# Dummy products on TensorE behind the key transposes, behind the counts of expert 0's search and ahead of the first list

## The reference

```
x = x + attention(layernorm(x), ctx, ctx)           # one head, D = 256, softmax over 256 keys
t = layernorm(x).reshape(4096, 256)
S = sigmoid(t @ Wg).T                               # 8 experts x 4096 rows
G, I = top_k(S, 1024)                               # each expert takes its 1024 best rows
hid = gelu(t[I] @ W1[e] + b1[e])                    # 256 -> 1024
out = (hid @ W2[e] + b2[e]) * G                     # 1024 -> 256
x = x + zeros.at[I].add(out)
```

## Time and profile before

| what | us |
|---|---|
| median of 3 runs (lowest, highest) | 510.77 (509.81, 510.78) |
| the profiled execution, its own time | 514.28 |
| its span in the trace | 512.5 |
| key transposes on TensorE start | 126.62 |
| first list written (`ids`) | 149.25 |
| first product of expert 0 on TensorE | 159.87 |
| first Gelu of expert 0 on ScalarE | 168.14 |

### The profile page before, as it was taken

The page is one execution under the profiler, slowest core; times in us unless marked ns, Lnnn a source line. Parts: engine busy times, 40 slices in busy tenths (PEclk is TensorE's granted clock), DMA queues, the critical chain, the costliest instruction groups (busy, mean ns, idle before and its releaser), DMA issues.

```text
span 512.5 us, 10717 instructions
## 1 busy us (share of the span) xinstructions
PE 481.5 (94%) x3806; PEld 347.7 (68%) x3807; DVE 334.1 (65%) x765; ACT 317.2 (62%) x607; POOL 287.0 (56%) x392
## 2 busy tenths in 40 slices
PE   7899999998357999999999999999999999999995
PEld 6688888877235558648747845864874784685484
DVE  6788999978874888675385465547538546535721
ACT  3777777866781782594387188259439618836920
POOL 1758999996324067546625726745662572773044
PEclk9999999999556999999999999999999999999998
DMA  7730766566803556547717916834761781683024
GB/s 223 234 114 2 232 179 165 142 187 182 241 16 100 178 126 104 103 130 136 139 35 202 163 22 194 171 48 135 137 132 52 188 160 22 187 105 41 2 33 50
DMA packets 91946, 64.21 MB, mean 125 GB/s; under 512 B 53060, under 2 KB 87816, under 8 KB 91912
## 3 DMA queue, kind: packets, MB, share of 16 engines
q1 hardware_dynamic: 78992, 46.41, 33.0%
q0 software_dynamic: 12288, 17.05, 20.9%
q10 hardware_dynamic: 632, 0.31, 0.2%
HBM read 35.83 MB, written 16.91 MB: 103 GB/s over the span
## 4 chain that ended last, share of the span: by engine, by line
PE 86%; DVE 5%; ACT 4%; issue 2%; DMA 1%; POOL 1%; POOLq 0%; SPq 0%; DVEq 0%; ACTq 0%
PE bank L1247 78%; PE bank L1254 2%; PE bank L1267 1%; DMA ctx<-in_ctx 1%; DVE cmp L931 1%; PE bank L1480 1%; ACT asign L665 1%; PE bank L1552 1%; PE bank L1274 1%; ACT g L683 1%; DVE oneh L1107 0%; DVE passed L942 0%; DVE cnt L940 0%; ACT xres L687 0%; PE bank L1350 0%
## 5 line engine op out<-in xcount | busy, mean ns | idle before, releaser
L1247 PE MATMUL bank<-w2h,xres 128*128 128x256 f16 x1024 | 169.4, 273 | 0.0
L1247 PE MATMUL bank<-exT,w1h 128*128 128x512 f16 (+1 forms) x528 | 155.3, 377 | 2.6 <-issue 2.6
L1247 PE MATMUL bank<-w2l,xres 128*128 128x256 f16 x512 | 139.5, 273 | 0.0
L517 POOL DMA_INDIRECT out<-yo,ids_s x64 | 100.6, 1572 | 48.6 <-issue 42.3
L1164 DVE TENSOR_TENSOR xres<-g,xres 128x512 f16<-128x512 f32 x128 | 87.7, 690 | 55.9 <-ACT xres L687 40.5
L1247 PEld LDWEIGHTS bank<-w2h,xres 128*128 128x128 f16 x1024 | 99.9, 98 | 12.3
L703 ACT ACTIVATE yo<-yt,ge 128x256 f32<-128x256 f32 x63 | 32.0, 508 | 116.2 <-DVE yt L1192 82.5
L683 ACT ACTIVATE g<-bank,b1e 128x512 f32<-128x512 f32 x128 | 88.2, 689 | 24.9 <-DVE b1e L1147 9.4
L1247 PE MATMUL bank<-exT,w1l 128*128 128x512 f16 (+1 forms) x264 | 99.5, 377 | 0.0
L1247 PEld LDWEIGHTS bank<-exT,w1h 128*128 128x128 f16 x528 | 51.7, 99 | 58.5 <-issue 2.8
L687 ACT ACTIVATE xres<-bank,b1e 128x512 f16<-128x512 f32 x128 | 87.5, 684 | 0.0
(11 more groups left out here) (249 smaller groups left out, 777.0 us busy)
## 6 DMA issues: line engine op xcount, KB each, us to landing
w2r<-in_L_ffn_W SPq DMA_DIRECT2D x8, 1024.0 KB
w1r<-in_L_ffn_W SPq DMA_DIRECT2D x8, 1024.0 KB
xres<-in_x SPq DMA_DIRECT2D x8, 512.0 KB, 5.5
out<-xres SPq DMA_DIRECT2D x4, 1024.0 KB, 7.2
ctx<-in_ctx SPq DMA_DIRECT2D x7, 512.0 KB, 4.6
rows_d<-xrow SPq DMA_DIRECT2D x7, 512.0 KB, 3.6
b_bc<-in_L_ffn_b SPq DMA_DIRECT2D x8, 128.0 KB, 3.6
ex<-rows_d,ids POOLq DMA_INDIRECT x64
```

Of the source, the lines that this page charges most:

```text
L517: pool.indirect_dma_start(out=rows_out, out_offset=bass.IndirectOffsetOnAxis(ap=ids_s[:, t:t + 1], axis=0), in_=yo[:, t, :], in_offset=Non ...
L1247: last = pe.matmul(out, lhs(a, c), rhs(b, c), start=i == 0, stop=i == len(terms) - 1)
```

## The change

`awake` is defined before the search instead of after it, and is called there: ten dummies ahead of the loop (right behind the key transposes), five behind every `fold(0, r)`, six behind `fold(1, 4)` (called `fold(1, Q1)` in the code) and six behind `slow_count(4)`, ahead of the list. That is 10 + 50 + 12 = 72 dummies more, beside the 23 that were there. Nothing else is changed; no other engine gets or loses an instruction.

```
+            def awake(times):
+
+                keep_awake(D_[:, 1, 0:2 * P], order16[:, 0:2].rearrange("p a k -> p (a k)"), times)
+
+            awake(10)
             for r in range(R1):
                 fold(0, r)
+                awake(5)
                 if r == 1:
                     fold(1, 0)
                 if r >= 4 and r % 2 == 0:
@@
                     slow_count((r - 3) // 2)
             ranks(0)
             fold(1, Q1)
+            awake(6)
             slow_count(4)
+            awake(6)
@@
-            def awake(times):
-
-                keep_awake(D_[:, 1, 0:2 * P], order16[:, 0:2].rearrange("p a k -> p (a k)"), times)
```

## The result

| | before | changed |
|---|---|---|
| median, us (lowest, highest; 12 runs each) | 510.73 (509.63, 511.39) | 511.93 (510.17, 512.93) |
| ratio to before, 95% interval | | 1.0026 (1.0016 to 1.0036) |
| profiled execution, us | 514.28 | 512.51 |
| last slow count, us behind the key transposes | 24.81 | 26.13 |

The change costs 1.2 us of the median, where +1.4 was forecast. The two profiled executions stand the other way round, 514.28 against 512.51, so a difference of their spans is no answer.

The account below looks back on a forecast made before the run. The selection's end was taken as held by TensorE's queue behind ScalarE-paced slow counts; 1.2 from the ten plus 0.55 from five, less 0.25 made good, gave about +1.4: 510.77 to 512.2 us, range 508.5 to 513.3.

Parts of the forecast that it names:

- the step: End of the list: its second half stands behind `slow_count(5)`, 1.45 late at 149.97, so `ids` and gathers come 1.4 late.
- The ten at the head: Ten dummies ahead of the search loop: at the low clock they make the first fold 1.2 late (bounds 0.1 and 1.2).
- rival 2: Search head: the clock never falls there, first fold only 0.1 late, slow counts 0.35; 511.1 us, chance 0.30.
- The five ahead of the first slow count: Search: five dummies delay the first slow count by 0.55, beside the search's shift of 1.2, 1.75 in all.
- The slow strand's +1.45: Search: every slow count after the first comes 1.45 late, as 0.25 is made good; bounds 0.35 and 2.4.
- The full clock given back: Search: clock up from 133 on saves some 0.09 in each of four rounds, so VectorE's strand is 0.85 late.
- rival 1: Search into expert 0: the clock stays up, first product 2.0 earlier, its count 1.1 sooner; -3.1, 507.7 us, chance 0.20.
- The first product at 161.3: Start of expert 0: predicted sign that its first product comes near 161.3, against 159.87 before.
- the step about the queue: Behind `slow_count(6)`: dummies, folds and transposes slide as a whole by 1.4; a first product by 159.87 would break it.

Follow-up runs that it names:

- e9: Kernel before with five dummies once, in round 3 between the fold and the first slow count: 511.31 us for 510.69, ratio 1.0014.
- e1: Changed kernel with the slow counts put ahead of the five dummies in rounds 3, 5, 7 and 9, all 72 kept: 511.11 us, ratio to before 1.0014.
- e8: Kernel before with the first four slow counts one round earlier in TensorE's queue, no dummies added: 509.87 us for 510.69, ratio 0.9979.
- e3: Kernel before with only the ten dummies ahead of the loop added: ratio to before 0.9988 (0.9978 to 0.9998).
- e7: Kernel before without the 23 old dummies behind the first list: ratio to before 0.9992 (0.9981 to 1.0002).
- e5: Kernel before with the second half of expert 0's list put ahead of `slow_count(5)`, no dummies added: ratio to before 1.0004 (0.9991 to 1.0017).
- e12: Changed kernel with slow counts ahead of the dummies, traced a second time, on a third chip: a single execution, no ratio; first product 33.53 us behind the key transposes.

## Why the prediction was right, and where it wasn't

- **Sign, size and the strand that carries them: right, the size partly by luck.** +1.2 measured for +1.4. The slow strand moved as a whole, `ids` came at 150.78 (forecast 150.7), held by `slow_count(5)` as the step had it, and the clock was at 0.50 again from 149 (forecast around 150). e9 (sufficient: five dummies ahead of one slow count make the kernel 0.6 slower) and e1 (taking the counts out from behind them gives 1.06 of the strand and 0.8 of the median back) show that the place in the queue does it; e8 shows it from the other side.
- **The ten at the head: the term was mis-sized.** 1.2 was taken; in the changed kernel's trace the first fold came 0.13 later by the span's time, and no later counted from the transposes. The clock hadn't fallen yet; e3 alone isn't slower. That was rival 2's condition and its sign (a first fold at 128.2), without rival 2's outcome, since the clock fell at 131.9, ahead of the first slow count.
- **The five ahead of the first slow count: mis-sized the other way.** 0.55 was taken, for a clock that has risen; it had fallen at 131.9 and the five took 1.04. The slow strand's +1.45 (its own figures give 1.75 - 0.26 = 1.49) looks met by +1.53 of span time at the last count, but 0.21 of that is a later start of the trace and 0.28 is between before's trace and e7's, without a dummy. What the change did is 1.04. So the strand's sum was 1.2 + 0.55 less what is made good, and the runs have nothing + 1.04: two errors of opposite sign. The rest of the median's +1.2 is what stays in e1, for which the forecast had no term.
- **The full clock given back: expected nowhere behind the list, and no gain over the kernels without the added dummies.** In 159 to 166 it is full, and rival 1's term for it came true: the last count comes 0.96 behind the first product (rival 1: 1.0; before's trace: 2.14). But e3 has the same (0.95), with only the ten added, and so has e8 (0.96) with none: there the old dummies are enough. Rival 1's -3.1 failed at its condition, as the clock fell at 149. TensorE finishes early, idles 1.87 (to 168.01), and falls to 0.50 at 169.4, inside expert 0.
- **The first product at 161.3: not met (159.58), and this isn't the step about the queue failing.** The second transposes start at 158.17, in before's trace at 156.65: 1.5 later, so the queue behind `slow_count(6)` did slide. Before's 159.87, the base of that sum, holds the late copy. Against e3's trace, with the same clock at the head and no late copy, the changed kernel's first product is 1.77 later (32.75 for 30.98) at a last slow count 1.03 later; the rest goes with the clock behind it, which rises at 155.8 in e3 and at 159.2 in the changed kernel.
- **Open:** the 0.45 to 0.7 us that stay with the slow counts ahead of the dummies (e1), whether of the fifty or the twelve; and the late copy.

## What to carry to other kernels

Dummy products cost time where something that another engine waits for stands behind them in TensorE's queue (and some was lost here even with the slow counts moved ahead, e1); a 3-column product with a whole strand behind it must stand ahead of the dummies, or better, where its operand is first ready (e8 gained 0.2% by that alone). And a higher clock is worth something only on the stretch where TensorE sets the end: here 72 dummies raised the granted clock from 5 or 6 to 7 or 8 tenths for 38 us and the kernel became slower, by 0.26%. Look first at which engine the end of the stretch waits for, and try the kernel without any dummies before adding more.

## What the runs showed of the hardware

- Waits without a known releaser, 1.8 to 4.9 us long, stand in all four traces of the chip on which before takes 514.77, in before's profiled execution (514.28), and in none of the eight traces of the two chips on which it takes 510.7. One of them, in before, lies between TensorE's last transpose in the rows (157.28) and ScalarE's copy (159.13). A sum made on such a trace should look for them first: the difference of two traces can be that of two chips.
- Whether the clock had fallen when the dummies began differed between executions of the same code: e5 and e7, alike up to there and on one chip, ran the key transposes in 0.69 and 0.44 us; and from the key transposes to the first fold, behind the ten dummies, e1 took 1.42 us, at full clock, and e12 2.52.
- The forecast quoted a rule of the Trainium skill ("TensorE: Matmul & The Clock Gate", "Why this matters for your kernels"), that the clock drops only behind long pauses. The changed kernel's trace is against it a second time: it fell at 149.0 with no pause over 1.66 us on TensorE, behind six dummies, sixteen list products and a wait.
